# Turning the first four batches' normalised rows by DMA instead of TensorE, in a decoder layer on one Trainium2 core

## The reference

```python
x = layernorm(x + attention(x))            # 32 heads of 16, causal
x = layernorm(x + cross_attention(x, ctx)) # 32 query heads, 8 key/value heads of 128, rope, mask
x = layernorm(x + ffn(x))                  # silu(x Wg) * (x Wu), then Wd; dequantised weights, inner width 1376
```

## Time and profile before

| | |
|---|---|
| median of 3 runs | 849.58 us (848.94 to 849.9) |
| time of the profiled execution | 849.92 us |
| its span, from first to last instruction | 848.1 us |
| PE busy | 827.7 us, 98% of the span |
| DVE busy | 689.2 us, 81% |
| POOL busy | 632.8 us, 75% |
| ACT busy | 533.6 us, 63% |
| chain that ended last | PE 62%, POOL 14%, DVE 7%, ACT 7%, issue 6%, DMA 3% |

### The profile page before, as it was taken

One profiled execution on the slowest core, in us unless ns is written; L12 is line 12 of the kernel. 1 busy time (PEld: TensorE's weight loads), 2 busy tenths in 40 slices (PEclk: granted clock), 3 DMA queues, 4 the chain that ended last, 5 costly groups with the idle time before them and its releaser, 6 DMA issues.

```text
span 848.1 us, 17377 instructions
## 1 busy us (share of the span) xinstructions
PE 827.7 (98%) x6125; PEld 465.5 (55%) x6125; DVE 689.2 (81%) x1077; ACT 533.6 (63%) x1560; POOL 632.8 (75%) x563
## 2 busy tenths in 40 slices
PE   9899999999999999999999999999999999999997
PEld 4677777655555554555555555555555644434444
DVE  5688788998688778689788788798889755899897
ACT  5798888554765666576575676665666753777400
POOL 1199999897676686578777677578888633999896
PEclk9999999999999999999999999999999999999999
DMA  7675255103244422434425125213442223230011
GB/s 192 194 256 181 63 160 163 54 18 108 38 95 130 112 39 75 112 39 138 105 38 155 33 40 161 38 26 91 133 93 39 46 42 105 72 110 20 2 48 52
DMA packets 120038, 76.76 MB, mean 91 GB/s; under 512 B 72877, under 2 KB 104336, under 8 KB 119952
## 3 DMA queue, kind: packets, MB, share of 16 engines
q1 hardware_dynamic: 117504, 74.86, 33.5%
q10 hardware_dynamic: 2448, 0.79, 0.5%
HBM read 52.50 MB, written 6.36 MB: 69 GB/s over the span
## 4 chain that ended last, share of the span: by engine, by line
PE 62%; POOL 14%; DVE 7%; ACT 7%; issue 6%; DMA 3%; SPq 0%; POOLq 0%; ACTq 0%; DVEq 0%
PE bank L356 16%; PE bank L358 16%; PE bank L357 16%; POOL rot L647 2%; POOL left L680 2%; PE bank L1667 2%; POOL q2l L653 2%; POOL pn L664 2%; ACT prob L845 2%; POOL prob L657 2%; PE bank L1840 1%; PE bank L1841 1%; PE bank L1760 1%; PE bank L1759 1%; PE bank L1758 1%
## 5 line engine op out<-in xcount | busy, mean ns | idle before, releaser
L657 POOL TENSOR_TENSOR prob<-prob,rden 128x512 f32<-128x512 f32 x64 | 67.8, 1060 | 103.3 <-DVE rden L1318 103.0
L647 POOL TENSOR_TENSOR rot<-rcos,rsin 128x512 f32<-128x512 f32 x80 | 106.5, 1332 | 20.3 <-DVE rsin L1260 19.8
L356 PE MATMUL bank<-aTh,xqh 128*128 128x512 f16 x256 | 97.1, 379 | 1.4 <-DVE rsin L1260 0.9
L356 PE MATMUL bank<-xoh,o2h 128*128 128x512 f16 x256 | 97.1, 379 | 0.1
L357 PE MATMUL bank<-xol,o2h 128*128 128x512 f16 x256 | 97.2, 379 | 0.0
L358 PE MATMUL bank<-xoh,o2l 128*128 128x512 f16 x256 | 97.1, 379 | 0.0
L357 PE MATMUL bank<-aTl,xqh 128*128 128x512 f16 x256 | 97.1, 379 | 0.0
L358 PE MATMUL bank<-aTh,xql 128*128 128x512 f16 x256 | 97.1, 379 | 0.0
L1010 ACT ACTIVATE prob<-bank,ebias 128x128 f32<-128x128 f32 x256 | 90.4, 365 | 2.1
L1260 DVE SCALAR_TENSOR_TENSOR rsin<-bank,sinq 64x512 f32<-64x512 f32 x128 | 88.1, 688 | 1.7
L664 POOL TENSOR_TENSOR pn<-prob,pn 128x512 f16<-128x512 f32 x64 | 84.1, 1315 | 6.8 <-ACT pn L1022 6.6
(11 more groups left out here) (224 smaller groups left out, 2652.7 us busy)
## 6 DMA issues: line engine op xcount, KB each, us to landing
tst<-tables SPq DMA_DIRECT2D x11, 768.0 KB, 5.2
xqs<-in_xwq SPq DMA_DIRECT2D x8, 1024.0 KB, 6.6
xos<-in_xwo SPq DMA_DIRECT2D x8, 1024.0 KB, 5.6
qst<-in_fq SPq DMA_DIRECT2D x11, 384.0 KB, 3.4
kstk<-stack SPq DMA_DIRECT2D x48, 64.0 KB, 2.3
qstk<-stack SPq DMA_DIRECT2D x21, 128.0 KB, 2.6
xs<-in_ctxT SPq DMA_DIRECT2D x2, 1024.0 KB, 6.3
res<-in_x SPq DMA_DIRECT2D x1, 2048.0 KB, 8.4
```

The costliest lines, as they stand in the source:

```text
L356: pe.matmul(out_ap, ah, bh, start=first, stop=False)
L647: nc.gpsimd.tensor_tensor(rot[:, r % 2, :], rcos[:, r % 2, :], rsin[:, r % 2, :], ALU.add).then_inc(rope_rot, 1)
L657: nc.gpsimd.tensor_tensor(prob[:, v % 2, :].rearrange("p (h k) -> p h k", h=QH), prob[:, v % 2, :].rearrange("p (h k) -> p h k", h=QH), rd ...
```

## The change

- `fill_plan()`: the four `"t"`, (0, b) fills of batches 0 to 3 are gone. The output projections stand in steps 52 to 55, `v` 0 in step 56, `k` 0 in step 57; from step 59 on nothing differs. `APPLY_SLOT` follows: steps 53 to 56.
- The norms of batches 0 to 3 are applied on ACT (`SHIFTED` now holds all eight), behind that step's `exps1` and `p1_hi`; right behind each, ACT rounds the rows into `rows` (`split_rows_hi`), a tile of three slots of 128 x 2 x 512 float16.
- DVE makes the low part (`split_rows_lo`) as the last thing of its step, behind the step's fill; both of its sources are in SBUF, where the removed `turned_lo` read one from PSUM.
- SP issues two DMA transposes per batch (`turn_rows`), eight in all, from `rows` into `aTh` and `aTl`, in its queue ahead of `load_o(1)`. The queries of half 0 wait for them (`rows_in`) in place of the fills.
- POOL makes `lnsh` for batches 0 to 3 too.

```diff
--- before.py
+++ after.py
@@ -64,9 +64,8 @@
 
 
 
-    plan = [(STEPS1 - 12, "k", (0,)), (STEPS1 - 11, "o", (0,)), (STEPS1 - 10, "o", (1,)), (STEPS1 - 9, "t", (0, 0))]
-    plan += [(STEPS1 - 9, "o", (2,)), (STEPS1 - 8, "t", (0, 1)), (STEPS1 - 8, "o", (3,)), (STEPS1 - 7, "t", (0, 2))]
-    plan += [(STEPS1 - 7, "v", (0,)), (STEPS1 - 6, "t", (0, 3))]
+    plan = [(STEPS1 - 12 + b, "o", (b,)) for b in range(BH)]
+    plan += [(STEPS1 - 8, "v", (0,)), (STEPS1 - 7, "k", (0,))]
     plan += [(STEPS1 - 5 + h, "q", (0, h)) for h in range(QH)]
     plan += [(STEPS1 - 1, "k", (1,)), (STEPS1, "v", (1,))]
     plan += [(STEPS1 + 1, "q", (1, 0)), (STEPS1 + 2, "q", (1, 1)), (STEPS1 + 3, "q", (1, 2)), (STEPS1 + 5, "q", (1, 3))]
@@ -146,7 +145,7 @@
 
 APPLY_SLOT = {(0, b): FILLS[find_fill("o", b)][0] + 1 for b in range(NB)}
 APPLY_SLOT.update({(1, b): T0 + BH * (BLOCK_OF[(G - 1, b // BH)]) + b % BH + 5 for b in range(NB)})
-SHIFTED = [(0, b) for b in range(BH, NB)]
+SHIFTED = [(0, b) for b in range(NB)]
 LATE_TURN = {APPLY_SLOT[(1, b)] + 1: b for b in range(BH, NB)}
 
 
@@ -229,7 +228,7 @@
         lnmv = sb("lnmv", [P, 3, 2], F32)
         lnve, lnrs = sb("lnve", [P, 3, 1], F32), sb("lnrs", [P, 3, 1], F32)
         power = sb("power", [P, 1], F32)
-        lnsh = sb("lnsh", [P, BH, 1], F32)
+        lnsh = sb("lnsh", [P, NB, 1], F32)
         scol16 = sb("scol16", [P, (NI - NSPLIT) * 2 * NK], F16)
         scol = sb("scol", [P, NI - NSPLIT, 2, NK], F32)
 
@@ -281,6 +280,9 @@
         o2h, o2l = at(20, "o2h", [P, 2, QH, S], F16), at(22, "o2l", [P, 2, QH, S], F16)
 
 
+        rows = at(155.5, "rows", [P, 3, 2, D], F16)
+
+
         qst = at(24, "qst", [P, 2, 3 * D], U16)
         tst = at(30, "tst", [P, 2, 2, 3 * D], F16)
         nib = at(42, "nib", [P, 3 * D], U16)
@@ -325,6 +327,7 @@
         oT_hi, oT_lo = sem("oT_hi"), sem("oT_lo")
         ln_sum, ln_stat, ln_aggr, ln_ve, ln_rs, ln_out = (
             sem("ln_sum"), sem("ln_stat"), sem("ln_aggr"), sem("ln_ve"), sem("ln_rs"), sem("ln_out"))
+        rows_hi, rows_lo, rows_in = sem("rows_hi"), sem("rows_lo"), [sem(f"rows_in{i}") for i in range(3)]
         ln_shift, ln_mid, ln_right = sem("ln_shift"), sem("ln_mid"), sem("ln_right")
         xt_hi, late_psum, late_hi, late_lo = sem("xt_hi"), sem("late_psum"), sem("late_hi"), sem("late_lo")
 
@@ -449,6 +452,13 @@
                 else:
                     sp.wait_ge(xo_lo, 4 * g)
                 sp.dma_start(xos[:, :, :], xwo.rearrange("(h p) n -> p h n", p=P)[:, g * QH:(g + 1) * QH, :]).then_inc(xo_in, 16)
+
+            def turn_rows(b):
+                if b == 0:
+                    sp.wait_ge(v1_psum, BLOCKS)
+                for i, (dst, done) in enumerate(((aTh, rows_hi), (aTl, rows_lo))):
+                    sp.wait_ge(done, b + 1)
+                    sp.dma_start_transpose(dst[:, :, b * S:(b + 1) * S], rows[:, b % 3, i, :]).then_inc(rows_in[b % 3], 16)
 
             def turn_probabilities(v):
                 sp.wait_ge(c_pn_lo, v + 1)
@@ -528,6 +538,8 @@
             load_q(1)
             stack_rows(7)
             load_kv(1)
+            for b in range(BH):
+                turn_rows(b)
             load_o(1)
             for t in range(STEPS1 - 8, END + 1):
                 if 1 <= t - T0:
@@ -723,7 +735,7 @@
 
             def inverse_sds(layer, t):
                 for (norm, b), slot in APPLY_SLOT.items():
-                    if norm == layer and slot == t + 1 and (norm, b) not in SHIFTED:
+                    if norm == layer and slot == t + 1 and (layer == 1 or slot < T0):
                         inverse_sd(layer * NB + b)
 
             for t in range(FIRST, END + 7):
@@ -833,6 +845,14 @@
                                      proj_bank(j, "v")[:, :].rearrange("p (b h d) -> p b h d", b=BH, h=HC),
                                      ACT.Copy, scale=2.0 ** (E_V1 - E_X - E_W)).then_inc(v1_hi, 1)
 
+            def split_rows_hi(b):
+                act.wait_ge(ln_out, b + 1)
+                if b == 0:
+                    act.wait_ge(v1_psum, BLOCKS - 1)
+                if b >= 3:
+                    act.wait_ge(rows_in[b % 3], 32 * (b // 3))
+                split_hi(rows[:, b % 3, 0, :], res[:, b, :], E_X).then_inc(rows_hi, 1)
+
             def exps1(u):
                 act.wait_ge(nmax_done, u + 1)
                 if u >= 2:
@@ -960,6 +980,12 @@
             for i, e in enumerate((E_QK, E_QK, E_V1)):
                 split_hi(bcols[:, i, :], bcol[:, i, :], e).then_inc(scaled_bias, 1)
             w1_split_hi(0, 2)
+            def scaled_norm(layer, b):
+                e, r = layer * NB + b, res[:, b, :]
+                act.wait_ge(ln_shift, SHIFTED.index((layer, b)) + 1)
+                nc.scalar.activation(r, r, ACT.Identity, scale=lnrs[:, e % 3, :],
+                                     bias=lnsh[:, SHIFTED.index((layer, b)), :]).then_inc(ln_out, 1)
+
             for t in range(FIRST, T0):
                 j, n = t // TILES1, t % TILES1
                 if j + 1 < BLOCKS and n == 4 and t > -TILES1:
@@ -971,6 +997,10 @@
                     seed_mask(t - STEPS1 + 2)
                 if 1 <= t <= STEPS1:
                     p1_hi(t - 1)
+                for layer, b in SHIFTED:
+                    if APPLY_SLOT[(layer, b)] == t:
+                        scaled_norm(layer, b)
+                        split_rows_hi(b)
                 if j + 2 < BLOCKS and n == 6:
                     k1_out_f32(j + 2)
                 if t == FIRST + 3:
@@ -992,12 +1022,6 @@
                 weight_pieces(t)
                 bank_splits([f for f in fills_at(t) if f not in turned_first(t)])
                 rotations(fills_at(t - 1))
-
-            def scaled_norm(layer, b):
-                e, r = layer * NB + b, res[:, b, :]
-                act.wait_ge(ln_shift, SHIFTED.index((layer, b)) + 1)
-                nc.scalar.activation(r, r, ACT.Identity, scale=lnrs[:, e % 3, :],
-                                     bias=lnsh[:, SHIFTED.index((layer, b)), :]).then_inc(ln_out, 1)
 
             def exps(v):
                 act.wait_ge(c_nmax, v + 1)
@@ -1238,6 +1262,10 @@
                 split_lo(aTl[:, :, b * S:(b + 1) * S], by_k(bank[f % 2][:, :]), aTh[:, :, b * S:(b + 1) * S],
                          E_X).then_inc(fill_free, 1)
 
+            def split_rows_lo(b):
+                dve.wait_ge(rows_hi, b + 1)
+                split_lo(rows[:, b % 3, 1, :], res[:, b, :], rows[:, b % 3, 0, :], E_X).then_inc(rows_lo, 1)
+
             def late_turned_lo(b):
                 dve.wait_ge(late_hi, b - BH + 1)
                 split_lo(aTl[:, :, b * S:(b + 1) * S], by_k(bank[4 + b % 2][:, :]), aTh[:, :, b * S:(b + 1) * S],
@@ -1461,6 +1489,9 @@
                 for f in fills_at(t):
                     if f not in turned_first(t):
                         consume(f)
+                for b in range(BH):
+                    if APPLY_SLOT[(0, b)] == t:
+                        split_rows_lo(b)
             for t in range(T0, END + 7):
                 v = t - T0
                 if 4 <= v < STEPS + 4:
@@ -1708,7 +1739,11 @@
                     if kind == "k" and n == 0:
                         pe.wait_ge(cT_lo, NHALF * NK)
                 if kind == "q":
-                    pe.wait_ge(fill_free, find_fill("t", 0, BH * ORDER[n][1] + BH - 1) + 1)
+                    if ORDER[n][1] == 0:
+                        for place in range(3):
+                            pe.wait_ge(rows_in[place], 32 * len(range(place, BH, 3)))
+                    else:
+                        pe.wait_ge(fill_free, find_fill("t", 0, NB - 1) + 1)
                     d = slice(what[1] * DK, (what[1] + 1) * DK)
                     last = project(dst[:, :], [xqh[:, i, k, d] for k in range(NK)], [xql[:, i, k, d] for k in range(NK)],
                                    aTh, aTl, cols)
```

## The result

The changed kernel takes 853.59 us (median of 5 runs, 851.96 to 854.33), the kernel before 849.58 (848.94 to 850.17, 5 runs beside it). The ratio is 1.0043, with an interval of 1.0031 to 1.0054: slower by 3.7 us, between 2.6 and 4.6 (the two medians lie 4.0 apart). The forecast was 852.0 with a range of 848.6 to 854.8. The profiled execution took 854.33 us, the longest of the five, with a span of 852.2, so 2.1 us lie around the span.

What follows compares the result with a forecast made beforehand. POOL's third query sum was taken to gate ACT and PE up to step 64; delays of +3.75 us end it at 194.3, tile 63 comes 2.5 late, rounded to +2.4 on 849.6: 852.0 us, range 848.6 to 854.8.

Steps and rivals of the forecast that it cites:

- What bounds: Up to step 64, POOL's third query sum gates ACT and PE; PE can gain at most 1.28 us.
- the closed loop: DVE steps 54 to 56: row maximum, exponentials, `pT`, norm, rounding, low part, next maximum; some 4.9 us each.
- PE's hole: PE waits for `pT` before weighing tile 55, some 4 us, from about 166 to 171.
- The price of the low part: DVE's low part with both sources in SBUF: taken as 1.0 us, between 0.68 and 1.79.
- The transposes: The last two DMA transposes land 3.1 us after the low part, at 173.0 us, just hidden before `q` (0, 0).
- The third rival: DMA transposes land late, up to 7.4 us; queries start 5.4 late, 855.0 us; chance 0.05.
- POOL's ledger: POOL's delays and savings up to the third query sum: +3.75 us, so it ends at 194.3 instead of 190.51.
- the old gap: POOL's one longer idle time before its third query sum, 1.53 us, was to disappear.
- the fourth rival: Behind PE's idle 4 us, `q` (0, 0)'s twelve matmuls run at half rate, 2.6 us more; 853.3 us; chance 0.06.
- the forecast mechanism: POOL's late third query sum makes tile 63 ready at 196.2, not 193.72: +2.4 us, 852.0; chance 0.40.
- the first rival: POOL catches up and it comes out even, within 0.2%: 849.0 to 851.3 us, say 850.4; chance 0.35.
- the second: Rival: PE keeps a lead and the kernel is faster by more than 0.2%, 847.8 us; chance 0.14.

Runs made afterwards that it cites:

- first experiment: Changed kernel plus 32 matmuls whose result nobody reads, ahead of the weighing of tile 55 where PE stood idle; 851.5 us, ratio 1.0018 to the kernel before.
- third experiments: Changed kernel with ACT's high part of `v` 0 put ahead of batch 3's norm in step 56; 850.88 us, ratio 1.0017 to the kernel before.
- second experiment: Changed kernel with DVE's low part moved to the next step, behind that step's row maximum and `pT`; 850.93 us, ratio 1.0016 to the kernel before.
- fifth experiments: Changed kernel with DVE's low part one step later and ACT's high part of `v` 0 ahead of batch 3's norm; 851.42 us, ratio 1.0018.
- fourth experiment: Changed kernel with fills in the old order: `k` 0 in step 52, output projections in 53 to 56, `v` 0 in 57; 856.6 us, ratio 1.0079.
- eighth experiment: Changed kernel with 32 unused matmuls in PE's idle time and POOL's last two `xos` weight pieces moved to steps 64 and 66; 850.53 us, ratio 1.0003.
- sixth kernel: Changed kernel with DVE's low part later, ACT's high part of `v` 0 first, and POOL's last two `xos` pieces in steps 64 and 66; 848.47 us, ratio 0.9974.

## Why the prediction was right, and where its size was off

**What bounds, and the closed loop: right.** Maxima of steps 53 to 57 were forecast at 148.16, 154.0, 158.9, 163.8 and 169.8 us. They came at 148.15, 155.27, 159.85, 164.55 and 170.23. The loops take 4.58 and 4.70 us against 4.9, the one with `v` 0 5.68 against 6.0, so each is 0.2 to 0.3 shorter than priced. The first is 1.3 late because POOL came out of its `xos` pieces at 151.58, not at 150.30. POOL's code ahead of that point is the same, so this is a chance of the execution: POOL ends those pieces 0.44 us behind step 53's transposes in before, 1.70 in after, and 0.45 and 1.24 in the traces of the first and third experiments. That the loop is what opens PE's hole is shown by the second, third and fifth experiments, which shorten it to 1.47, 3.17 and 0.60.

**The price of the low part: near its lower bound.** The four took these times (all instructions on the tile `rows` of after, min/median/max in ns, and their transposes to landing in us):

```profile
L1179 DVE SCALAR_TENSOR_TENSOR rows<-res,rows x4: 681/693/894, 154.5 to 169.6; 128x512 f16<-128x512 f32 x4
...
DMA to landing us min/median/max: 2.4/2.4/2.6
```

I had taken 1.0 between bounds of 0.68 and 1.79. Three of four are at the bound, and in one case it was POOL that had to wait: its cast at 169.75 takes 1.03 instead of 0.61, while the fourth low part runs. In other orders the same instruction took 1.39, 1.43 and 1.28 (fourth and second experiments), so values well over 1.0 do occur; here two of the four fell on POOL's three short instructions, one of which, a `lnsh`, took 0.47 for it instead of 0.27.

**PE's hole: right.** Some 4 us was forecast, 3.77 measured. `q` (0, 0) was to start at 173.0 and started at 174.35. Of this 1.35, 0.95 is slow clock: from 172.38 on, the transposes, the output's transpose and the scores take 0.91, 0.21 and 0.85 us from start to start, against 0.47, 0.11 and 0.44 at full clock. The twelve small matmuls of the weighing at 171.57 lose next to nothing, 0.31 us from first to last start against 0.28.

**The transposes: hidden, as forecast.** They land 2.4 us after issue, not 3.1: the last was issued at 170.34 and is there 1.6 us before `q` (0, 0). The third rival did not come. The fourth experiment shows the same transfer in the open, after 2.5 us.

**POOL's ledger: right in the sum, by partly other terms.** Forecast 194.3 for the third query sum, measured 194.47, or 3.96 us over 190.51. By the rows: the late start 1.3, the old gap gone -1.53, new gaps 0.98 and 1.56 (I had 0.92 and 2.8), four `lnsh` 1.24 from start to next start (1.06), the blocked cast 0.42 (0.5). Sum 3.97. The shorter loops made up what the late start took. From run to run this term moves: in the first experiment the same queue is only 2.54 later.

**The step that was mis-sized: the clock.** I gave the fourth rival 0.06 and left it out of the sum. It happened, with numbers near those worked out for it: `q` (0, 0)'s matmuls behind the hole took twice as long, for nine of twelve, +1.90 us against 2.6. What I had not priced is the small work ahead of it, +0.95. With these 2.85 us of clock PE comes to tile 63 4.32 later, and POOL's 2.7 is hidden behind that. Without them PE would be 1.5 later, and POOL's sum would have set the end at 196.4, as the forecast said (196.2). The first experiment takes the clock loss away, and the ratio falls from 1.0043 to 1.0018. So the runs split the 3.7 us into about 1.5 for the forecast mechanism (I said 2.4) and about 2.1 for the rival that I took for unlikely. The forecast landed 1.6 us low by the medians because one term was too large and another missing. That the two errors partly cancel, and that the number lies as near as it does, is luck: in the profiled execution what ended last at tile 63 was PE with its slow clock and not POOL's sum, on which the forecast rested., from which I worked it out, showed the two speeds; what should have raised the chance is that I forecast a hole of 4 us myself, with no row of a hole that PE left at full clock. The Trainium skill's rule that an idle array falls back to its lower clock (TensorE: Matmul & The Clock Gate, section What's actually happening) agrees with the windows of after, 0.63 and 0.68 from 170 to 180.

**The other rivals.** An even result (the first rival, within 0.2%) and a faster one (the second) lie outside the interval. The second has its reason in the rows: PE did not keep its lead, because POOL idled 2.54 us and PE itself 3.77.

**What stays open.** The clock fell in or behind holes of 3.77, 3.17, 3.12, 2.28 and 1.47 us, not behind 1.29, 1.29 and 1.06. The length of the hole alone does not decide it: in the eighth experiment's trace PE stood still for 2.07 us, up to 72.09, far ahead of the seam, and the granted clock stayed at 1.00 in every window from 60 to 85. These are single traces, and the clock differs from one execution of a kernel to the next: the mean over the execution goes from 0.994 to 1.000 among the eleven counted of the second experiment, so in one of them it can hardly have fallen at the seam. Why 1.47 was enough in the second experiment's trace, and why the slow stretch lasted until 178.2 in one kernel and until 173.6 in another with almost the same hole, no run tells: the work between holes differs as well (from 165 to 170 PE is busy 3.36 us in the second experiment, 3.94 in the sixth). The sixth kernel's remaining 1.06 and 1.29 us were not attacked.

## What to carry to other kernels

Before a low part, a copy or any consumer of another engine is put at the end of an in-order step, ask whether that engine's input for the next step is made by the instruction behind it: here each step became a loop of 4.6 to 4.7 us, although DVE had 2.2 us less work in all. When a forecast contains a hole in TensorE of several microseconds, price the matmuls behind it at the lower clock as the default, not as a rival: at this seam the clock was down behind every unfilled hole from 1.47 us up. A gain of the critical engine that does not show in the time may be held back by the next queue: the change came to a ratio of 0.9974 with DVE's order, ACT's order and POOL's weight pieces moved along with it, while the last of these alone gave 1.0002.

## What the hardware showed that was not expected

- 32 useless matmuls in PE's hole make the kernel about 2.1 us faster (ratio 1.0018 in place of 1.0043, 0.9 to 3.4 us by the intervals): a full clock behind the hole is worth more than the work costs.
- A hole of 1.47 us was followed in the second experiment's trace by a clock of 0.50 over the window from 170 to 175, behind a window in which PE was busy 3.36 of 5 us. In the fifth a wait of 2.28 us was followed by matmuls of 0.63 us as well.
- A 128x512 float16 transpose by DMA from SBUF to SBUF lands in 2.4 us in the median (2.6 at most in the changed kernel, 4.2 in the fourth), with 1.2 to 1.3 us on SP's queue for the issue; the `pT<-pn` ones took 3.0 at the least and 3.1 in the median.
- VectorE's low part, which reads two operands from SBUF, and POOL slow each other, and which of them loses changes with the order: the low part took up to 1.43 us instead of 0.68, POOL's cast up to 1.16 instead of 0.61.
